# Turning each gathered tile once, in place, in a routed expert layer on one NeuronCore

## The chip, the cores and the metric

One NeuronCore of a Trainium2 chip runs the whole program. The metric is the device time of one execution in microseconds (us). PE is TensorE, DVE VectorE, ACT ScalarE, POOL GpSimd, and SP the queue that issues most DMAs.

## The reference

x has the shape (32, 32, 256), all float32. Each of the 32 sequences picks a 32x32 matrix by its index and is mixed by it; the 1024 tokens of width 256 that come out (y) go through a mixture of experts, and the result is added to x.

```python
w = weights[conditions]                        # 200 matrices of 32x32, one picked per sequence
y = einsum('bct,bcd->bdt', x, w)               # 1024 tokens, width 256
probs = softmax(y @ w_router)                  # 16 experts
top_w, top_i = top_k(probs, 4); top_w /= sum(top_w)
g = silu(y @ we1[e]) * (y @ we3[e])            # each chosen expert, hidden width 128
moe = sum over the 4 of  top_w * (g @ we2[e])
shared = silu(y @ ws1) * (y @ ws3) @ ws2       # hidden width 512
out = x + shared / 5 + moe * 4 / 5
```

## The kernel before

**Routing.** y is computed, the experts' logits and the four choices per token are found, and every (token, choice) gets a slot in an order sorted by expert. The 4096 slots make 32 *tiles* of 128 rows. POOL gathers them, `xs[:, j, :]` for tile j, by one indirect DMA each (L433) from y in DRAM (`y_of`). A tile may hold rows of several experts, so the work goes by *items*: an item is a tile with one expert, and there are 47 of them in the tiles' order, run in 24 pairs. The tile and the expert of an item are known only at run time (`item_t_i`, `item_e_i`), so engines load them into registers (`load`, a TENSOR_LOAD in the profile) and address by register.

**The loop of pairs.** All engines run `for i in range(PAIRS + LAG)` (27 rounds) with a pipeline by round. Pair n's steps, and the lines at which the profile shows them:

- SP copies the two gathered tiles of an item pair from `xs` into a ring `xt` of three pairs (`copy_pair`, L372), 128 KB each, addressed by register; for pairs 0 and 1 ACT does this (L526). Item j of a tile that has several experts copies that tile again.
- PE transposes each copied tile (`turn_pair`, L945, two 128x128 blocks a tile) into `xt_ps`, a PSUM bank for each of two pairs, in round n (t_turned).
- ACT copies x to `x_hi` in a reduced float format (L541), and DVE computes `x_lo = x - x_hi` (L752), in round n. The first four pairs (PLAIN) use x as it is, in buffers `x_f`.
- PE multiplies with the expert's two first weights (gate and up), in three products of high and low parts (L992; L986 for plain pairs), in round n + 1; ACT takes silu of the gate (L545) and DVE multiplies it by up (L757).
- In round n + 3 PE transposes that product (L970), ACT copies it to `gt` (L537), PE multiplies with the second weight (L1008, "down"), and DVE adds the rows that belong to the item into `merged` (L786, a register address each).

`merged` and `xs` are views of one store: tile m of `merged` lies on tile m - 16 of `xs`. DVE clears two tiles of `merged` a round from round 4 to 15 (L767). POOL scatters each finished tile of `merged` to DRAM (L440) after all gathers are issued.

**Weights.** Each expert's gate and up weights are loaded into `raw`, then ACT makes the high part (L466) and DVE the low part (L605, w_lo), in the order of ORDER; `SPLIT` and `HI_BEHIND` say behind which round. The last four units, 16 to 19, reuse buffers of the plain experts. Their loads are behind the copies of pairs 8, 9, 11 and 13 in SP's queue (LOAD_BEHIND), and each waits for `t_gate_up` 4, which is when the plain rounds are over.

**Gates.** POOL's gather of tile j waits until pair (j - LEAD) // 2 - 1 is turned, with LEAD 6. In rounds 17 and 18 ACT also writes four diagonal matrices each (L552), which PE uses at the end.

**After the loop.** PE does two more units of the shared expert (L894, L907); SP loads the scattered results back by token once the last scatter has landed; ACT, DVE and PE weigh and add them, and the output is stored.

In the loop the order on each engine is that of the code: PE has turn, transposed product, gate/up, down; ACT has gt, x, silu, weight; DVE has x_lo, g, weight, clear, merge.

Of the kernel before, what the change touches and what calls it, by code (L numbers as in the profile page):

```python
# [16 lines left out]
P = 128  # L17
# [3 lines left out]
def adaln_ffn(nc, x, itok, cond_w, w_router, we1, we3, we2, ws1, ws3, ws2, out):  # L21
# [21 lines left out]
    RING = 3  # L43
    LAG = 3
    SRING = 4
# [4 lines left out]
    LEAD = 6  # L50

    EARLY = 2

    LOAD_BEHIND = {8: UNITS - 2, 9: UNITS - 1, 11: UNITS, 13: UNITS + 1}


# [4 lines left out]
    LO_FRONT = [15, 2, 3, 4, 5, 6, 7, 8]  # L61
# [15 lines left out]
    with ExitStack() as ctx:  # L77
# [19 lines left out]
        xt = sb("xt", [P, RING, 2, D])  # L97
# [42 lines left out]
        def early(first, tiles):  # L140
# [32 lines left out]
        raw_at = ([xt[:, k, :, :].rearrange("p i d -> p (i d)") for k in range(FRONT)] + [raw[:, k, :] for k in range(E - LATE)]  # L173
                  + [xt[:, FRONT, :, :].rearrange("p i d -> p (i d)")] + [raw[:, k, :] for k in range(4)])
# [72 lines left out]
        xt_out = sem("xt_out")  # L247
        xt_in = [sem(f"xt_in{r}") for r in range(RING)]
        t_cleared = sem("t_cleared")
        t_turned = sem("t_turned")  # L250
        t_x_hi = sem("t_x_hi")
# [72 lines left out]
        def _(sp):  # L324
# [29 lines left out]
            registers = {}  # L354

            def copy_pair(n):

                if n == EARLY or n % 6 == 0:
                    some = range(2 * n, 2 * (n // 6 + 1) * 6)
                    values = [sp.alloc_register(f"tile{j}") for j in some]  # L360
                    sp.wait_ge(items_done, 1)
                    sp.load(values, item_t_i[0:1, some[0]:some[-1] + 1])
                    registers.update({j: sp.snap(v, donate=True, min_val=0, max_val=TILES - 1) for j, v in zip(some, values)})
                if n >= RING:
                    sp.wait_ge(t_turned, n - RING + 1)
                else:
                    sp.wait_ge(dve_lo, n + 1)
                for i in range(halves(n)):
                    j = 2 * n + i
                    if j < TILES:  # L370
                        sp.wait_ge(tile_in[j % TT], 16 * (j // TT + 1))
                    sp.dma_start(xt[:, n % RING, i, :],  # L372
                                 xs[:, bass.ds(registers[j], 1), :].rearrange("p a d -> p (a d)")).then_inc(xt_in[n % RING], 16)
# [72 lines left out]
        def _(act):  # L446
# [71 lines left out]
            registers = [act.alloc_register(f"early{j}") for j in range(2 * EARLY)]  # L518
            act.wait_ge(items_done, 1)
            act.load(registers, item_t_i[0:1, 0:2 * EARLY])  # L520
            tiles = [act.snap(v, donate=True, min_val=0, max_val=TILES - 1) for v in registers]
# [48 lines left out]
        def _(dve):  # L570
# [150 lines left out]
            low(LO_FRONT[0])  # L721
            gated(3)
            for n in LO_FRONT[1:]:
                low(n)
# [23 lines left out]
            for i in range(PAIRS + LAG):  # L748
                if (n := pair_at(i, 0)) is not None and n >= PLAIN:
# [18 lines left out]
                if i % 6 == 1 and (first := 2 * (i - 1)) < ITEMS_UP:  # L768

                    registers = [dve.alloc_register(f"merge{first + n}") for n in range(12)]  # L770
                    dve.wait_ge(items_done, 4)
                    dve.load(registers, item_t_i[0:1, first:first + 12])
# [280 lines left out]
```

## Time and profile before

| | |
|---|---|
| time, median of 3 runs | 149.15 us (148.77 to 152.94) |
| profiled execution | 150.12 us, of which the span of instructions is 148.4 us |
| TensorE clock granted, mean over the span | 0.976 |
| busy: PE / DVE / ACT / POOL | 135.7 / 105.4 / 70.5 / 65.9 us |
| loop of pairs, from the first transposes to the last merge | some 43 to 121 us |

The span runs from the first to the last instruction; what the time has beyond it lies around the program. An engine is busy while an instruction of its own runs; issuing a DMA and loading a register are not counted as busy. The chain is the row of work that ended last, followed back from the end.

### The profile page before, as it was taken

The page shows a single profiled execution, that of the slowest core. Times are in us where ns is not written, and L with a number is a line of the kernel's source. Part 1 is how long each engine was busy: PE and PEld are TensorE (multiplying, and loading weights), DVE is VectorE, ACT ScalarE, POOL GpSimd, SP SyncE. Part 2 cuts the span into 40 slices and gives each one's busy share as a digit, 9 for nine tenths or more (in the row PEclk, how much of TensorE's full clock was granted, in tenths as well). Part 3 has the DMA queues.
Part 4 walks back from the last instruction along what each step waited for, and adds up shares of the span by engine and source line. Part 5 has one row for each costly group of instructions (what it writes and reads, how often), then busy time and mean ns, then how long its engine had stood idle before and what let it go on. Part 6 is the DMA issues. An engine that isn't in the chain of part 4 may idle for free.

```text
span 148.4 us, 2809 instructions
## 1 busy us (share of the span) xinstructions
PE 135.7 (91%) x816; PEld 115.7 (78%) x816; DVE 105.4 (71%) x274; ACT 70.5 (47%) x162; POOL 65.9 (44%) x79
## 2 busy tenths in 40 slices
PE   5999999899889999998799999999999999995920
PEld 3459978688677789997799999999999878884810
DVE  4175777997939997775988989766766551119992
ACT  4046248999354544435344544485543221198000
POOL 3400000003778777775557766776576774000000
PEclk9999959999999999999999999999999999999995
DMA  3659989995335667788767665555432222799324
GB/s 99 224 139 254 261 273 289 352 328 163 104 108 172 207 176 192 208 248 274 210 200 204 228 215 173 190 198 186 175 110 106 81 101 106 247 410 414 130 71 141
DMA packets 22413, 29.55 MB, mean 199 GB/s; under 512 B 2912, under 2 KB 19168, under 8 KB 22272
## 3 DMA queue, kind: packets, MB, share of 16 engines
q1 hardware_dynamic: 18848, 19.67, 40.5%
q0 software_dynamic: 3120, 8.52, 19.0%
q10 hardware_dynamic: 432, 1.20, 2.3%
q8 instruction: 7, 0.11, 0.4%
q14 instruction: 6, 0.05, 0.1%
HBM read 17.45 MB, written 6.29 MB: 160 GB/s over the span
## 4 chain that ended last, share of the span: by engine, by line
PE 59%; DVE 14%; DMA 11%; POOL 5%; issue 4%; ACT 2%; DVEq 1%; POOLq 1%; SPq 0%
PE up_ps L992 17%; PE down_ps L1008 12%; PE down_ps L831 6%; PE gate_ps L945 6%; PE up_ps L986 4%; POOL store_t L433 3%; PE down_ps L970 3%; DMA raw<-in_L_ffn_we 3%; DMA raw<-result 3%; DMA xt<-store_t 2%; PE down_ps L849 2%; DVE acc L804 2%; ACT raw L557 2%; DMA store_t<-y_of,token_i 2%; PE down_ps L856 2%
## 5 line engine op out<-in xcount | busy, mean ns | idle before, releaser
L433 POOL DMA_INDIRECT store_t<-y_of,token_i x32 | 31.7, 992 | 43.1 <-DVE token_i L704 30.0
L440 POOL DMA_INDIRECT result<-store_t,back_i x32 | 31.4, 980 | 12.9 <-DVE store_t L786 7.4
L786 DVE SCALAR_TENSOR_TENSOR store_t<-down_ps,valid,store_t 128x256 f32 x47 | 21.5, 458 | 8.8 <-DVE store_t L786 4.9
L992 PE MATMUL up_ps<-w_hi,x_hi 128*128 x78 | 23.6, 303 | 1.2 <-DVE x_lo L752 1.2
L1008 PE MATMUL down_ps<-w,gt 128*128 x94 | 24.5, 381 | 0.0
L992 PE MATMUL up_ps<-w_hi,x_lo 128*128 x78 | 22.0, 282 | 0.0
L992 PE MATMUL up_ps<-w_lo,x_hi 128*128 x78 | 22.0, 282 | 0.0
L537 ACT ACTIVATE gt<-down_ps 128x256 f32<-128x256 f32 (+1 forms) x24 | 9.1, 379 | 20.6 <-PE down_ps L970 19.4
L1008 PEld LDWEIGHTS down_ps<-w,gt 128*128 128x128 f32 x94 | 16.3, 190 | 1.9 <-issue 0.5
L545 ACT ACTIVATE sil<-up_ps 128x256 f32<-128x256 f32 (+1 forms) x24 | 9.1, 379 | 16.1 <-PE up_ps L992 11.4
L992 PEld LDWEIGHTS up_ps<-w_hi,x_hi 128*128 128x128 f32 x78 | 14.8, 189 | 1.5 <-issue 1.5
L992 PEld LDWEIGHTS up_ps<-w_hi,x_lo 128*128 128x128 f32 x78 | 14.8, 190 | 0.0
L992 PEld LDWEIGHTS up_ps<-w_lo,x_hi 128*128 128x128 f32 x78 | 14.8, 189 | 0.0
L945 PE MATMUL gate_ps<-ident,xt 128*128 128x128 f32 x94 | 14.2, 273 | 0.5 <-DMA xt<-store_t 0.5
L752 DVE TENSOR_TENSOR x_lo<-gate_ps,x_hi 128x512 fp32r<-128x512 f32 (+1 forms) x20 | 13.4, 671 | 1.6 <-ACT x_hi L541 1.1
L945 PEld LDWEIGHTS gate_ps<-ident,xt 128*128 128x128 f32 x94 | 11.7, 141 | 3.3 <-DMA xt<-store_t 0.9
L605 DVE TENSOR_TENSOR w_lo<-raw,w_hi 128x512 fp32r<-128x512 f32 x17 | 11.1, 691 | 1.4 <-ACT w_hi L466 1.3
L757 DVE TENSOR_TENSOR g<-sil,up_ps 128x256 f32<-128x256 f32 (+1 forms) x24 | 9.8, 410 | 3.1 <-ACT sil L545 3.1
L620 DVE TENSOR_TENSOR g<-sil,up_ps 128x512 f32<-128x512 f32 x8 | 5.5, 684 | 8.9 <-PE up_ps L894 6.6
L541 ACT ACTIVATE x_hi<-gate_ps 128x512 fp32r<-128x512 f32 (+1 forms) x20 | 11.7, 583 | 0.0
L466 ACT ACTIVATE w_hi<-raw 128x512 fp32r<-128x512 f32 x17 | 10.1, 620 | 1.1 <-DMA raw<-in_L_ffn_we 1.1
L831 PE MATMUL down_ps<-sil 128*128 128x512 f32 x16 | 8.7, 707 | 1.5 <-DVE sil L571 1.5
(154 smaller groups left out, 244.8 us busy)
## 6 DMA issues: line engine op xcount, KB each, us to landing
xt<-store_t SPq DMA_DIRECT2D x43, 128.0 KB
raw<-in_L_ffn_we SPq DMA_DIRECT2D x30, 128.0 KB, 3.4
w<-in_L_ffn_we SPq DMA_DIRECT2D x4, 512.0 KB, 6.8
raw<-result SPq DMA_DIRECT2D x4, 512.0 KB, 5.1
w_lo<-result SPq DMA_DIRECT2D x4, 512.0 KB, 8.2
acc<-in_x SPq DMA_DIRECT2D x2, 512.0 KB, 4.3
y_of<-store_t ACTq DMA_DIRECT2D x1, 1024.0 KB, 6.1
out<-acc SPq DMA_DIRECT2D x3, 256.0 KB, 2.1
```

Source lines behind the costliest of these rows:

```text
L433: pool.indirect_dma_start(xs[:, j, :], None, y_of, bass.IndirectOffsetOnAxis(ap=token_i[:, j:j + 1], axis=0),).then_inc(tile_in[j % TT], 16)
L440: pool.indirect_dma_start(result, bass.IndirectOffsetOnAxis(ap=back_i[:, j:j + 1], axis=0), merged[:, j, :], None,).then_inc(result_out[j ...
L466: act.activation(high_of(n), raw_at[n], ACT.Copy).then_inc(act_hi, 1)
L541: act.activation((x_hi[:, b, :, :] if n >= PLAIN else x_f[b])[:, 0:m, :], xt_ps[b][:, 0:m, :], ACT.Copy).then_inc(t_x_hi, 1)
L605: dve.tensor_tensor(low_of(n), raw_at[n], high_of(n).bitcast(F32), ALU.subtract).then_inc(dve_lo, 1)
L752: dve.tensor_tensor(x_lo[:, b, 0:m, :], xt_ps[b][:, 0:m, :], x_hi[:, b, 0:m, :].bitcast(F32), ALU.subtract).then_inc(t_x_lo, 1)
L757: dve.tensor_tensor(t_gated[:, b, 0:m, :], t_sil[:, b, 0:m, :], gu_ps[b][:, 0:m, H:2 * H], ALU.mult).then_inc(t_g, 1)
L786: dve.scalar_tensor_tensor(out=into, in0=out_ps[n % 2][:, h, :], scalar=valid[:, it:it + 1], in1=into, op0=ALU.mult, op1=ALU.add).then_inc ...
L831: pe.matmul(row_ps[0][:, :], warm[:, 0:P], warm, start=True, stop=True)
L945: last = pe.transpose(xt_ps[b][:, h, k * P:(k + 1) * P], xt[:, r, h, k * P:(k + 1) * P], ident[:, :])
L992: last = pe.matmul(gu_ps[b][:, h, :], (x_hi, x_lo)[a][:, b, h, k * P:(k + 1) * P], pair_of(w, experts[h], k), start=(m == 0), stop=(m == 3 ...
L1008: last = pe.matmul(out_ps[b][:, h, :], gt[:, b, h, :], w2_of(experts[2 + h]), start=True, stop=True)
```

## The change

PE now transposes each gathered tile once, straight out of `xs`, two tiles a time (TURNS = 16 pairs of tiles), one pair ahead of the loop: `turn_pair(0)` and `turn_pair(1)` before it, `turn_pair(i + 1)` in round i up to round 14. ACT copies the turned pair back over the gathered tiles (`keep`, in `xs`). x_hi, x_f and x_lo are then taken from `xs` for each item by register: two operations of 128x256 on ACT and two on DVE for a pair, instead of one of 128x512 each. SP's copies, ACT's early copies and the ring `xt` go; its room becomes `first_raw`. ACT loads 12 tile registers before the loop and at the ends of rounds 5, 11 and 17; DVE loads its 12 at the starts of rounds 0, 6, 12 and 18 instead of inside rounds 1, 7, 13 and 19. The four late weights are loaded directly behind the second weights in SP's queue. LEAD becomes 10, and three weight splits on DVE (LO_FRONT) go ahead of the g of shared step 3.

```diff
-    RING = 3
     LAG = 3
+    TURNS = TILES // 2
+    GROUP = 6
...
-    LEAD = 6
-
-    EARLY = 2
-
-    LOAD_BEHIND = {8: UNITS - 2, 9: UNITS - 1, 11: UNITS, 13: UNITS + 1}
+    LEAD = 10
...
-    LO_FRONT = [15, 2, 3, 4, 5, 6, 7, 8]
+    LO_FRONT = [15, 2, 3, 4]
+    LO_THEN = [5, 6, 7, 8]
...
+        def x_of(t):
+            return xs[:, bass.ds(t, 1), :].rearrange("p a d -> p (a d)")
...
-            for n in range(EARLY, PAIRS):
-                copy_pair(n)
-                if n in LOAD_BEHIND:
-                    load(LOAD_BEHIND[n])
+            for n in range(UNITS - 2, UNITS + 2):
+                load(n)
...
+            def load_tiles(i):
+                registers = [act.alloc_register(f"turned{2 * i + j}") for j in range(2 * GROUP)]
+                act.load(registers, item_t_i[0:1, 2 * i:2 * (i + GROUP)])
+                tiles.extend(act.snap(r, donate=True, min_val=0, max_val=TILES - 1) for r in registers)
+
+            def keep(n):
+                act.wait_ge(t_turned, n + 1)
+                act.activation(xs[:, 2 * n:2 * n + 2, :], xt_ps[n % 2], ACT.Copy).then_inc(t_kept, 1)
+
             act.wait_ge(items_done, 1)
-            act.load(registers, item_t_i[0:1, 0:2 * EARLY])
...
-            for n in range(EARLY):
-                act.wait_ge(dve_lo, n + 1)
-                for j in range(2 * n, 2 * n + 2):
-                    act.wait_ge(tile_in[j], 16)
-                    act.activation(xt[:, n, j % 2, :], xs[:, bass.ds(tiles[j], 1), :].rearrange("p a d -> p (a d)"), ACT.Copy).then_inc(xt_out, 1)
+            load_tiles(0)
+            keep(0)
             for n in HI_BEHIND[-1]:
                 high(n)
...
                 if (n := pair_at(i, 0)) is not None:
-                    b, m = n % 2, halves(n)
-                    act.wait_ge(t_turned, n + 1)
-                    act.activation((x_hi[:, b, :, :] if n >= PLAIN else x_f[b])[:, 0:m, :], xt_ps[b][:, 0:m, :], ACT.Copy).then_inc(t_x_hi, 1)
+                    act.wait_ge(t_kept, min(n + 1, TURNS))
+                    for h in range(halves(n)):
+                        act.activation((x_hi[:, n % 2, :, :] if n >= PLAIN else x_f[n % 2])[:, h, :], x_of(tiles[2 * n + h]), ACT.Copy).then_inc(t_x_hi, 1)
+                if i + 1 < TURNS:
+                    keep(i + 1)
...
+                if i % GROUP == GROUP - 1 and i + 1 < PAIRS:
+                    load_tiles(i + 1)
...
-            low(LO_FRONT[0])
+            for n in LO_FRONT:
+                low(n)
             gated(3)
-            for n in LO_FRONT[1:]:
+            for n in LO_THEN:
                 low(n)
...
             for i in range(PAIRS + LAG):
+                if i % GROUP == 0 and i < PAIRS:
+                    registers = [dve.alloc_register(f"merge{2 * i + j}") for j in range(2 * GROUP)]
+                    dve.wait_ge(items_done, 4)
+                    dve.load(registers, item_t_i[0:1, 2 * i:2 * (i + GROUP)])
...
                 if (n := pair_at(i, 0)) is not None and n >= PLAIN:
-                    b, m = n % 2, halves(n)
-                    dve.wait_ge(t_x_hi, n + 1)
-                    dve.tensor_tensor(x_lo[:, b, 0:m, :], xt_ps[b][:, 0:m, :], x_hi[:, b, 0:m, :].bitcast(F32),
-                                      ALU.subtract).then_inc(t_x_lo, 1)
+                    for h in range(halves(n)):
+                        dve.wait_ge(t_x_hi, 2 * n + h + 1)
+                        dve.tensor_tensor(x_lo[:, n % 2, h, :], x_of(tiles[2 * n + h]), x_hi[:, n % 2, h, :].bitcast(F32),
+                                          ALU.subtract).then_inc(t_x_lo, 1)
...
-                    dve.wait_ge(t_turned, i + 1)
...
             def turn_pair(n):
-                r, b = n % RING, n % 2
-                if n < EARLY:
-                    pe.wait_ge(xt_out, 2 * n + 2)
-                else:
-                    pe.wait_ge(xt_in[r], 16 * (2 * (n // RING - (r < EARLY)) + halves(n)))
+                b = n % 2
+                for h in range(2):
+                    pe.wait_ge(tile_in[(2 * n + h) % TT], 16 * ((2 * n + h) // TT + 1))
                 if n < 2:
                     pe.wait_ge(silu_done, STEPS - 1 + n)
-                for h in range(halves(n)):
+                else:
+                    pe.wait_ge(t_kept, n - 1)
+                for h in range(2):
                     for k in range(KD):
-                        last = pe.transpose(xt_ps[b][:, h, k * P:(k + 1) * P], xt[:, r, h, k * P:(k + 1) * P], ident[:, :])
+                        last = pe.transpose(xt_ps[b][:, h, k * P:(k + 1) * P], xs[:, 2 * n + h, k * P:(k + 1) * P], ident[:, :])
                 last.then_inc(t_turned, 1)
...
             turn_pair(0)
             down(3)
+            turn_pair(1)
             for i in range(PAIRS + LAG):
-                if (n := pair_at(i, 0)) is not None and n:
-                    turn_pair(n)
+                if 0 < i < TURNS - 1:
+                    turn_pair(i + 1)
```

## Rows read from the trace of the kernel before

**Rows 1.** The page, the chain that ended last, share of the span by engine.

```profile
PE 59%; DVE 14%; DMA 11%; POOL 5%; issue 4%; ACT 2%; DVEq 1%; POOLq 1%; SPq 0%
```

**Rows 2.** The chain in order of time (start, us, what): one settled round, round 24's start.

```profile
88.60 0.44 PE gate_ps L945 x4
89.04 0.22 PE down_ps L970 x2
89.26 1.43 PE up_ps L992 x12
90.68 0.87 PE down_ps L1008 x4
...
114.92 0.22 PE down_ps L970 x2
```

**Rows 3.** PE's timeline: start, us, instructions, and in brackets idle time before and releaser.

```profile
48.51 0.66 PE L945 MATMUL gate_ps<-ident,xt 128*128 128x128 f32 x4 [0.52 <-DMA xt<-store_t]
...
54.88 1.89 PE L986 MATMUL up_ps<-raw,g 128*128 x8
...
71.32 0.38 PE L992 MATMUL up_ps<-w_hi,x_hi 128*128 x1 [1.23 <-DVE x_lo L752]
```

**Rows 4.** The chain in order of time: the two DMAs behind those waits.

```profile
44.95 3.52 DMA xt<-store_t
...
63.07 4.00 DMA raw<-in_L_ffn_we
```

**Rows 5.** Busy time in PE's round 9: stretch, its length, each engine, clock, DMA.

```profile
69.27:73.71 4.44, 3.21 (x24) 2.82 (x23) 3.83 (x9) 1.54 (x4) 2.51 (x3) 1.00 0.74 227
```

**Rows 6.** DVE's timeline: the g of step 3, then from one x_lo to the next.

```profile
43.09 0.69 DVE L620 TENSOR_TENSOR g<-sil,up_ps 128x512 f32<-128x512 f32 x1 [2.25 <-PE down_ps L907]
...
70.49 0.68 DVE L752 TENSOR_TENSOR x_lo<-gate_ps,x_hi 128x512 fp32r<-128x512 f32 x1
71.09 0.41 DVE L757 TENSOR_TENSOR g<-sil,up_ps 128x256 f32<-128x256 f32 x1
...
72.93 0.68 DVE L752 TENSOR_TENSOR x_lo<-gate_ps,x_hi 128x512 fp32r<-128x512 f32 x1
```

**Rows 7.** Groups by line and shape: busy us, mean ns of one, idle before.

```profile
L605 DVE TENSOR_TENSOR w_lo<-raw,w_hi 128x512 fp32r<-128x512 f32 x17 | 11.1, 691 | 1.4 <-ACT w_hi L466 1.3
L757 DVE TENSOR_TENSOR g<-sil,up_ps 128x256 f32<-128x256 f32 x23 | 9.6, 416 | 3.1 <-ACT sil L545 3.1
L526 ACT ACTIVATE xt<-store_t 128x256 f32 x4 | 1.5, 412 | 3.0 <-DVE valid L719 2.4 <-DMA store_t<-y_of,token_i 0.6
```

**Rows 8.** ACT's timeline: the first late weight, then round 17's diagonals, gt and x.

```profile
67.09 0.63 ACT L466 ACTIVATE w_hi<-raw 128x512 fp32r<-128x512 f32 x1 [1.05 <-DMA raw<-in_L_ffn_we]
...
96.89 1.26 ACT L552 ACTIVATE store_t<-ident,top_w 128x128 f32<-128x128 f32 x4
98.13 0.39 ACT L537 ACTIVATE gt<-down_ps 128x256 f32<-128x256 f32 x1
98.41 0.59 ACT L541 ACTIVATE x_hi<-gate_ps 128x512 fp32r<-128x512 f32 x1
```

**Rows 9.** Register loads by line: four registers on ACT, twelve on DVE (ns min/median/max).

```profile
L520 ACTq TENSOR_LOAD <-item_t_i x1: 501/501/501, 39.6 to 39.6; - x1
...
L772 DVEq TENSOR_LOAD <-item_t_i x4: 1005/1162/1520, 48.5 to 102.9; - x4
```

**Rows 10.** The gathers: tile 9's in POOL's timeline, and all landings by line L433.

```profile
47.35 0.95 POOL L433 DMA_INDIRECT store_t<-y_of,token_i  x1 [0.30 <-issue]
...
DMA to landing us min/median/max: 2.7/3.4/5.3
```

**Rows 11.** POOL's timeline: three of the scatters.

```profile
83.12 1.23 POOL L440 DMA_INDIRECT result<-store_t,back_i  x1 [0.30 <-issue]
...
115.82 0.97 POOL L440 DMA_INDIRECT result<-store_t,back_i  x1 [0.50 <-DVE store_t L786]
...
123.47 0.97 POOL L440 DMA_INDIRECT result<-store_t,back_i  x1 [0.30 <-issue]
```

More of the change, by code:

```diff
@@ L96, in adaln_ffn @@
         raw = sb("raw", [P, E - LATE, WC])
-        xt = sb("xt", [P, RING, 2, D])
+        first_raw = sb("first_raw", [P, FRONT + 1, WC])
         w_2 = sb("w_2", [P, E + FRONT, D])
@@ L170, in adaln_ffn @@
             "p (m n) -> p m n", m=4)
-        raw_at = ([xt[:, k, :, :].rearrange("p i d -> p (i d)") for k in range(FRONT)] + [raw[:, k, :] for k in range(E - LATE)]
-                  + [xt[:, FRONT, :, :].rearrange("p i d -> p (i d)")] + [raw[:, k, :] for k in range(4)])
+        raw_at = ([first_raw[:, k, :] for k in range(FRONT)] + [raw[:, k, :] for k in range(E - LATE)]
+                  + [first_raw[:, FRONT, :]] + [raw[:, k, :] for k in range(4)])
         x_f = [v[:, :, HALF - D:HALF] for v in (sil, g)]
@@ L246, in adaln_ffn @@
         tile_in = [sem(f"tile_in{r}") for r in range(TT)]
-        xt_out = sem("xt_out")
-        xt_in = [sem(f"xt_in{r}") for r in range(RING)]
         t_cleared = sem("t_cleared")
         t_turned = sem("t_turned")
+        t_kept = sem("t_kept")
         t_x_hi = sem("t_x_hi")
@@ L353, in _ @@
                 sp.dma_start(w_2[:, e, :], we2[e].rearrange("e h d -> h e d")).then_inc(w_2_in, 16)
[L354 to L365, printed above, removed]
-                else:
[L367 to L373, printed above, removed]
-            for n in range(EARLY, PAIRS):
-                copy_pair(n)
-                if n in LOAD_BEHIND:
-                    load(LOAD_BEHIND[n])
+            for n in range(UNITS - 2, UNITS + 2):
+                load(n)
             sp.wait_ge(dve_lo, turn[FRONT + 4] + 1)
@@ L516, in _ @@
                         zero(m)
-            registers = [act.alloc_register(f"early{j}") for j in range(2 * EARLY)]
-            act.wait_ge(items_done, 1)
-            act.load(registers, item_t_i[0:1, 0:2 * EARLY])
-            tiles = [act.snap(v, donate=True, min_val=0, max_val=TILES - 1) for v in registers]
-            for n in range(EARLY):
-                act.wait_ge(dve_lo, n + 1)
-                for j in range(2 * n, 2 * n + 2):
-                    act.wait_ge(tile_in[j], 16)
-                    act.activation(xt[:, n, j % 2, :], xs[:, bass.ds(tiles[j], 1), :].rearrange("p a d -> p (a d)"), ACT.Copy).then_inc(xt_out, 1)
+            tiles = []
+            def load_tiles(i):
[5 more added lines that the diff above has]
+                act.activation(xs[:, 2 * n:2 * n + 2, :], xt_ps[n % 2], ACT.Copy).then_inc(t_kept, 1)
+            act.wait_ge(items_done, 1)
+            load_tiles(0)
+            keep(0)
             for n in HI_BEHIND[-1]:
@@ L748, in _ @@
             for i in range(PAIRS + LAG):
+                if i % GROUP == 0 and i < PAIRS:
+                    registers = [dve.alloc_register(f"merge{2 * i + j}") for j in range(2 * GROUP)]
+                    dve.wait_ge(items_done, 4)
+                    dve.load(registers, item_t_i[0:1, 2 * i:2 * (i + GROUP)])
+                    tiles += [dve.snap(r, donate=True, min_val=0, max_val=TILES - 1) for r in registers]
                 if (n := pair_at(i, 0)) is not None and n >= PLAIN:
-                    b, m = n % 2, halves(n)
-                    dve.wait_ge(t_x_hi, n + 1)
-                    dve.tensor_tensor(x_lo[:, b, 0:m, :], xt_ps[b][:, 0:m, :], x_hi[:, b, 0:m, :].bitcast(F32),
-                                      ALU.subtract).then_inc(t_x_lo, 1)
+                    for h in range(halves(n)):
+                        dve.wait_ge(t_x_hi, 2 * n + h + 1)
+                        dve.tensor_tensor(x_lo[:, n % 2, h, :], x_of(tiles[2 * n + h]), x_hi[:, n % 2, h, :].bitcast(F32),
+                                          ALU.subtract).then_inc(t_x_lo, 1)
                 if (n := pair_at(i, 1)) is not None:
@@ L764, in _ @@
                 if ZEROED <= i < TILES // 2:
-                    dve.wait_ge(t_turned, i + 1)
                     dve.memset(merged[:, 2 * i:2 * i + 2, :], 0.0).then_inc(t_cleared, 1)
[L768 to L772, printed above, removed]
-                    tiles += [dve.snap(r, donate=True, min_val=0, max_val=TILES - 1) for r in registers]
                 if (n := pair_at(i, LAG)) is not None:
@@ L974, in _ @@
                     if n < PLAIN:
-                        pe.wait_ge(t_x_hi, n + 1)
+                        pe.wait_ge(t_x_hi, 2 * n + halves(n))
                     else:
-                        pe.wait_ge(t_x_lo, n - PLAIN + 1)
+                        pe.wait_ge(t_x_lo, 2 * (n - PLAIN) + halves(n))
                     if n == PLAIN:
```

1 line of the change is left out of this document (removed).

## The prediction

> **What bounds the kernel now.** I read the page's chain first, then the chain in order of time over the loop of item pairs, then each engine's timeline in a few rounds, and last the tail. PE carries the chain for 59% of the span [rows 1]. In the loop a settled round on the chain is four transposes of x (0.44 us), two of the gated product (0.22), twelve gate/up matmuls (1.43) and four down matmuls (0.87): 2.95 us, with nothing between them [rows 2]. So a round costs what PE executes in it, and what leaves PE leaves the round, until another engine takes over. Two waits break this: 0.52 us before the transposes of pair 2, and 1.23 us before the gate/up of pair 8 [rows 3]. The first ends with a row copy that took 3.52 us to land, the second with a late expert weight whose load was issued only at 63 us [rows 4]; that round took 4.44 us [rows 5] instead of 2.95. DVE has little room: where it waits for no other engine it needs 2.44 us from one split of x to the next [rows 6], and in rounds 7, 9, 12 and 14 it splits a weight as well.
>
> **The change, part by part.** Round i means pass i of the loop.
>
> *Fewer transposes.* There are 47 items in 23.5 pairs, but 32 tiles in 16 pairs. Each pair turned costs 0.44 us of PE [rows 2], so 7.5 pairs fewer give 3.3 us. It falls in the rounds from 15 on, which become 2.95 - 0.44 = 2.51 us; before that PE does the same four transposes a round, one pair earlier.
>
> *No row copies.* SP's 43 copies go, and with them the 0.52 us in front of pair 2 [rows 3]. What is late next at that place is the gather itself: PE now turns pair i+1 in round i and so needs tile 2i+3. Tile 9, whose gather starts at 47.35, lands 2.7 to 5.3 us later [rows 10], at 50.1 to 52.7. PE wants it in round 3, near 50.8: the 48.51 of now, less 0.52, plus one more pair (0.44), a plain gate/up (1.89) [rows 3] and another pair (0.44). At the median landing of 3.4 PE waits almost nothing, at the worst 2 us, and once: two gathers are issued in 2.5 us, a round is longer. I take nothing, and keep 0 to 2 for the range. POOL's gate is loosened too (LEAD 10): at 1.25 apart, with a few longer ones, the 22 gathers after tile 9 are through near 77 us. Nobody waits for SP in the loop any more but for late weights.
>
> *Late weights at once.* They now wait only for the end of the plain gate/ups (54.88 + 1.89, [rows 3]) and for their buffers' splits, not behind the copies of pairs 8 to 13. Eight issues at some 0.4 us each and 4.0 to land [rows 4] bring the first unit at about 61.5 and the last near 64; ACT first wanted one at 66.0 [rows 8]. The 4.44 - 2.95 = 1.5 us [rows 2, 5] go. Their 1 MB now meets the gathers of rounds 5 to 7, which by then have about 1 us of lead; that is within the 0 to 2 above.
>
> *VectorE at the loop's start.* Three weight splits move ahead of the g of step 3. DVE sat idle there for 2.25 us until PE's down was done [rows 6], and three splits take 2.1 at 0.69 [rows 7]: covered. Without that cover PE's last down would start up to 2.1 later. ACT now waits for the first transposes with the high part of unit 10 queued behind; that is read two splits later.
>
> Gross gain: 3.3 + 0.5 + 1.5 = 5.3 us. Against it stand the new steps on ACT and DVE.
>
> *ScalarE.* It gains the copy of each turned pair from PSUM in place, a 128x512 like the x copy of now, 0.59 [rows 8], and its one x copy becomes two from SBUF with a register address: L526 is that operation, at 0.41 us [rows 7]. Issue to issue such a copy takes between 0.28 [rows 8] and that; I take 0.34. A round's work is 0.28 + 0.68 + 0.59 + 0.28 = 1.83 against 2.95. By order: the product's transposes end 0.66 into PE's round, then come their copy, two parts, the kept copy and silu, which ends near 2.75. Behind the new wait on t_turned are queued silu, which DVE's g waits for, and in some rounds a weight copy; the next round's copy is wanted at 3.6, so all of it is hidden. A load of 12 registers is bounded by 0.5 (four on ACT) and 1.0 to 1.5 (twelve on DVE) [rows 9], I take 1.1; in rounds 5 and 11 it fits. In rounds 17 and 18 it doesn't: PE's rounds are 2.51 there, ACT has 1.24 for copies and silu, 1.26 for four diagonals [rows 8], and in 17 the load. The copy that down(15) waits for comes about 0.5 us late. Bounds: 0 and 1.5.
>
> *VectorE.* The split of x (0.60 from issue to issue [rows 6]) becomes two of 128x256, each with its own wait and register operation. Its price lies between 0.30 each, half of the old one, and 0.42, the duration of g at that size [rows 7], plus 0.11 for the register operation: 0 to 0.46 more a round. DVE runs behind PE there, so its queue is filled and these steps overlap; I take 0.11, near the low end, so a round of 2.55. The load of 12 registers now stands right before the split of x. It takes 1.0 to 1.5 [rows 9], of which the merge still running covers 0.4; I take 0.7. From the split of pair 6 to that of pair 16, ten rounds: 25.5, four weight splits at 0.69 [rows 7] 2.8, the routing weights 0.7, one load 0.7: 29.7 us. PE's time between the gate/ups of these pairs: eight rounds of 2.95, two of 2.51, less 0.44, since no turning stands ahead of the last: 28.2. At pair 6 DVE is some 0.7 ahead (silu ends 2.75 into a round and the merges start 0.5 into the next; 1.0 for them, load 0.7, split 0.7: 2.9 against the 3.6 at which PE wants it). So PE waits 29.7 - 28.2 - 0.7 = 0.8 us in rounds 13 to 16. With the bounds' ends: none, or 4 to 5.
>
> By the Trainium skill, DMA: Bandwidth & Descriptors, "Latency and other measured facts", a tensor load has a floor near 600 ns. The rows agree for four registers (501 ns) but show about twice that for twelve [rows 9], so the rows are used; at the page's figure most of DVE's load would be covered, and the gain would be some 0.5 larger.
>
> *Net:* 5.3 - 0.5 - 0.8 = 4.0 us.
>
> **Does the tail keep it?** After the loop the end hangs on POOL's last scatter, the loads of the results and DVE's sums. POOL last waited for a merge at 115.82, 0.9 after round 24 began [rows 2, 11], and then issued six more, 1.275 apart. Round 24 comes 4.0 earlier, so this moves as a whole, and the shared steps with it. POOL's own floor is 77 + 31 x 1.275 = 116.5 for the last issue, 7 us ahead of 123.47 [rows 11]; it doesn't bind at a gain of 4.
>
> The profiled execution took 150.12 us, 148.4 of it the span; minus 4.0 it gives 146.1. The median of the runs, 149.15, lies 1.0 lower, so I forecast 145.1.
>
> **Rivals.**
> - *Nothing new waits*: DVE's and ACT's steps stay covered; 149.15 - 5.3 = 143.8. For it: ACT's 1.83 and DVE's 2.55 are under a round. Against: DVE's weight splits and loads come on top.
> - *DVE becomes the bound* in rounds 6 to 16: the halves don't overlap (0.46 more a round, not 0.11) and a load costs 1.1. That is 10 x 0.35 + 0.4 = 3.9 on top of the forecast: 149.0; half of it, 147. For it: each half has its own wait and address. Against: a register operation fits beside the instruction that is running.
> - *The split of x slows POOL* (the other side). x's split now reads two inputs from SBUF instead of one from there and one from PSUM. The only operation of that kind in the loop is the weight split; the scatter beside one, at 83.12, took 1.23 us instead of 0.97 [rows 11]. If every scatter lost 0.35, the last would be issued at 77 + 31 x 1.625 = 127.4, 3.9 later than now: 153. It decides from a pitch of 1.50, (123.47 - 77)/31. Against: the gather at 47.35, beside weight splits too, took its usual 0.95 [rows 10]. The Trainium skill, SBUF — State Buffer, "Who interferes with whom", has such a rule: a VectorE instruction with two SBUF inputs contends with a GpSimd instruction that reads SBUF. By that rule the time would go this way; the trace agrees in one of these two rows.
> - *Gathers are late*: PE waits up to 2 us in rounds 2 to 7: 147.
>
> **How the numbers follow.** The forecast's own case (144 to 146.1): 0.52. Nothing new waits: 0.13. DVE the bound, or gathers at full price: 0.27. POOL slowed: 0.08. Two per cent is 3 us (146.2 and 152.1), about what can be told from no change here. Of the third case nearly all lies between these. Faster 0.65, same 0.27, slower 0.08. Range: from 143.3 (no new wait, and 0.5 of the median's own spread) to 148.5, which leaves out the dearest part of the DVE case and POOL's.
>
> **What would show it.** 64 transposes of x, none after round 14; rounds of 2.95 before and about 2.5 after; no wait for a weight at pair 8; PE waits for x_lo in rounds 13 to 16 and for gt at 18; the last scatter issued near 119.5. It is wrong if x's halves take clearly more than 0.35 from issue to issue, if PE's transposes wait for gathers, or if scatters stand over 1.3 us apart without waiting for a merge.

## The result, and the profile after

The changed kernel takes **147.14 us** (median of 4 runs, 146.93 to 151.51) beside 149.27 for the kernel before in the same comparison: a ratio of **0.9864, 95% interval 0.9824 to 0.9903**. (All ratios here leave out executions of either kernel that the chip had disturbed.) So it is faster, clear of the noise, but by 2.1 us where the forecast said 4.0. The time lies inside the range, but above 146.2; it is among the cases "within 2%". Measured twice more, on other chips, the same kernel gave ratios of 0.991 and 0.9885 (below), so the gain is 1.4 to 2.1 us.

The profiled execution took 147.29 us, 145.2 of it the span. The page's chain, which answers to [rows 1]: TensorE's share fell from 59% to 52%, VectorE's rose from 14% to 26%.

```profile
PE 52%; DVE 26%; issue 7%; DMA 4%; ACT 3%; DVEq 2%; POOL 1%; POOLq 1%; ACTq 0%; SPq 0%
```

The chain in order of time (start, us, what), for [rows 2 and 3]. The four transposes (L928) end with round 14; a round of 2.95 us (60.36 to 63.31) becomes one of 2.52 (108.73 to 111.25). Before the transposes of pair 3 (tiles 6 and 7) there is a new wait of 0.95 us.

```profile
47.45 0.95 issue
48.40 0.63 PE gate_ps L928 x4
...
60.36 0.44 PE gate_ps L928 x4
60.80 0.22 PE down_ps L954 x2
61.02 1.43 PE up_ps L976 x12
62.44 0.87 PE down_ps L992 x4
63.31 0.44 PE gate_ps L928 x4
...
108.73 0.22 PE down_ps L954 x2
108.95 1.44 PE up_ps L976 x12
110.38 0.87 PE down_ps L992 x4
111.25 0.22 PE down_ps L954 x2
```

The chain calls this wait "issue", because the profile names no releaser for it. The gather's own rows show what ended it (by line L408, tile 7 alone): it was issued at 43.49 and landed 4.82 us later, at 48.31. The transposes of pair 3 start 0.09 behind that, at 48.40.

```profile
L408 POOL DMA_INDIRECT store_t<-y_of,token_i x1: 1342/1342/1342, 43.5 to 43.5; - x1
...
DMA to landing us min/median/max: 4.8/4.8/4.8
```

Stretches of TensorE's rounds 6 and 9 (length, busy time of PE, PEld, DVE, ACT, POOL, clock, DMA share, GB/s), for [rows 5]: round 9 is now 2.94 long, where it was 4.44.

```profile
60.36:63.31 2.95, 2.95 (x25) 2.79 (x23) 2.09 (x7) 1.81 (x5) 2.32 (x3) 1.00 0.89 248
...
69.20:72.14 2.94, 2.94 (x25) 2.78 (x23) 2.68 (x8) 2.25 (x6) 2.33 (x3) 1.00 0.33 109
```

VectorE's timeline, for [rows 6]. With nothing to wait for, it needs 2.51 us from one split of x to the next (68.48 to 70.99; the forecast took 2.55). At 80.92 it stands 0.77 us: the registers of round 12 are being loaded.

```profile
68.48 0.75 DVE L742 TENSOR_TENSOR x_lo<-store_t,x_hi 128x256 fp32r<-128x256 f32 x2
...
70.99 0.75 DVE L742 TENSOR_TENSOR x_lo<-store_t,x_hi 128x256 fp32r<-128x256 f32 x2
...
80.92 0.76 DVE L742 TENSOR_TENSOR x_lo<-store_t,x_hi 128x256 fp32r<-128x256 f32 x2 [0.77 <-issue]
...
92.22 0.75 DVE L742 TENSOR_TENSOR x_lo<-store_t,x_hi 128x256 fp32r<-128x256 f32 x2
```

By line, for [rows 9 and 10] (ns or us, min/median/max): VectorE's and ScalarE's register loads, and the gathers' landings.

```profile
L737 DVEq TENSOR_LOAD <-item_t_i x4: 849/953/1099, 42.3 to 96.6; - x4
...
L497 ACTq TENSOR_LOAD <-item_t_i x4: 782/792/967, 38.6 to 94.9; - x4
...
DMA to landing us min/median/max: 2.6/2.9/5.3
```

GpSimd's scatters, for [rows 11]. Before, GpSimd still waited for a merge at 115.82, six scatters from the end. Now its last real wait is at 89.38; 24 scatters follow, 1.28 us apart with 0.30 idle between them, to the last. Two of them, at 94.48 and 110.01, took 1.18 and 1.22 instead of 0.97, so that the next came 1.5 behind.

```profile
83.71 0.97 POOL L415 DMA_INDIRECT result<-store_t,back_i  x1 [1.52 <-DVE store_t L769]
...
89.38 0.97 POOL L415 DMA_INDIRECT result<-store_t,back_i  x1 [0.87 <-DVE store_t L769]
90.66 0.97 POOL L415 DMA_INDIRECT result<-store_t,back_i  x1 [0.30 <-issue]
...
94.48 1.18 POOL L415 DMA_INDIRECT result<-store_t,back_i  x1 [0.30 <-DVE store_t L769]
95.97 0.97 POOL L415 DMA_INDIRECT result<-store_t,back_i  x1 [0.30 <-issue]
...
110.01 1.22 POOL L415 DMA_INDIRECT result<-store_t,back_i  x1 [0.31 <-issue]
...
120.45 0.97 POOL L415 DMA_INDIRECT result<-store_t,back_i  x1 [0.30 <-issue]
```

Both stand beside a split of x, which now reads both of its inputs from SBUF (VectorE's timeline):

```profile
94.40 0.75 DVE L742 TENSOR_TENSOR x_lo<-store_t,x_hi 128x256 fp32r<-128x256 f32 x2
...
109.96 0.42 DVE L742 TENSOR_TENSOR x_lo<-store_t,x_hi 128x256 fp32r<-128x256 f32 x1
```

**Where the gain went.** The stage ahead of the loop varies by some 1.3 us from one execution to the next (last section), so I measure from the loop's first transposes (L928, at 41.81 here, 42.79 before). The transposes of the gated product in round 24 stand 69.27 us behind them, before 71.96; the last scatter stands 78.64 behind, before 80.68. The loop gives 2.69 up to round 24 instead of 4.0, and 0.65 of that is lost between round 24 and the last scatter (9.37 us, before 8.72). What is left, 2.04, is close to the 2.1 of the medians.

### The profile page after: what moved, and what is told of

Read it like the earlier page. It is cut to its first block, busy times and chain, and to the rows that moved or that the text cites. A ratio compares the mean times of both kernels' runs of the same rounds, so it can differ in the third digit from the quotient of the medians.

```text
span 145.2 us, 2793 instructions
## 1 busy us (share of the span) xinstructions
PE 132.2 (91%) x786; PEld 111.6 (77%) x786; DVE 105.9 (73%) x293; ACT 78.8 (54%) x197; POOL 67.1 (46%) x79
## 4 chain that ended last, share of the span: by engine, by line
PE 52%; DVE 26%; issue 7%; DMA 4%; ACT 3%; DVEq 2%; POOL 1%; POOLq 1%; ACTq 0%; SPq 0%
PE up_ps L976 13%; PE down_ps L992 10%; PE down_ps L814 6%; PE down_ps L890 5%; PE up_ps L970 5%; PE gate_ps L928 3%; DVE store_t L769 3%; DMA raw<-result 3%; PE down_ps L954 2%; PE down_ps L832 2%; DVE acc L787 2%; ACT raw L541 2%; DVE x_lo L742 2%; DVE store_t L756 2%; DMA result<-store_t,back_i 2%
## 5 line engine op out<-in xcount | busy, mean ns | idle before, releaser
L408 POOL DMA_INDIRECT store_t<-y_of,token_i x32 | 32.5, 1014 | 38.5 <-DVE token_i L688 29.0
L742 DVE TENSOR_TENSOR x_lo<-store_t,x_hi 128x256 fp32r<-128x256 f32 x39 | 14.8, 420 | 2.2 <-ACT x_hi L521 1.3
L521 ACT ACTIVATE x_hi<-store_t 128x256 fp32r x39 | 14.0, 408 | 0.0
L502 ACT ACTIVATE store_t<-gate_ps 128x512 f32<-128x512 f32 x16 | 9.4, 590 | 6.8 <-PE gate_ps L928 6.8
L814 PE MATMUL down_ps<-sil 128*128 128x512 f32 x16 | 9.3, 747 | 1.5 <-DVE sil L555 1.5
L928 PE MATMUL gate_ps<-ident,store_t 128*128 128x128 f32 x64 | 9.5, 273 | 0.9 <-issue 0.9
```

The source lines that it names most:

```text
L408: pool.indirect_dma_start(xs[:, j, :], None, y_of, bass.IndirectOffsetOnAxis(ap=token_i[:, j:j + 1], axis=0),).then_inc(tile_in[j % TT], 16)
L521: act.activation((x_hi[:, n % 2, :, :] if n >= PLAIN else x_f[n % 2])[:, h, :], x_of(tiles[2 * n + h]), ACT.Copy).then_inc(t_x_hi, 1)
L742: dve.tensor_tensor(x_lo[:, n % 2, h, :], x_of(tiles[2 * n + h]), x_hi[:, n % 2, h, :].bitcast(F32), ALU.subtract).then_inc(t_x_lo, 1)
L814: pe.matmul(row_ps[0][:, :], warm[:, 0:P], warm, start=True, stop=True)
L928: last = pe.transpose(xt_ps[b][:, h, k * P:(k + 1) * P], xs[:, 2 * n + h, k * P:(k + 1) * P], ident[:, :])
```

## The experiments

Theory, before these runs: the four microseconds were there, and three new waits took half: gathers that land late, VectorE in rounds 12 to 17, GpSimd's own pace at the end. Rivals: the late weights at once were needed for the gain in round 9; the split of x slows GpSimd; the tail keeps whatever the loop gains. All kernels but one (the late weights alone) start from the changed one. "R24" and "last" are the distances of round 24's transposes and of the last scatter from the loop's start, in the profiled execution (changed kernel 69.27 and 78.64).

**Turning behind gate and up.** It gives every gather some 1.65 us more, the 0.22 and 1.43 of the steps that now stand ahead.

```diff
-                if 0 < i < TURNS - 1:
-                    turn_pair(i + 1)
...
                     last.then_inc(t_gate_up, 1)
+                if 0 < i < TURNS - 1:
+                    turn_pair(i + 1)
```

> The changed kernel, with PE turning the next pair of tiles after the gate/up of a round instead of ahead of it, and ACT keeping it after silu. Theory: the 0.95 us that PE stands before the turning of pair 3 is the gather of tile 7, which the change asks for one pair sooner than it lands; with the gate/up of pair 1 in front the gather has time, the wait goes, every later round and scatter starts earlier by it: 146.3 us, 0.8 below the changed kernel. Rival: the wait is absorbed later anyway, since DVE is late in rounds 12 to 16: 147.1, no change.

Ratio 0.9968 (0.9925 to 1.0011), R24 69.78: in time nearly all of the gain is gone, though to round 24 its profile is only 0.5 behind the changed kernel's; the loop also starts 0.97 later in this profile (last section). No wait at pair 3 (8.16 us to round 3 instead of 9.38, with one turning, 0.44, fewer in it), but now rounds 9, 11, 12, 13, 14 and 16 are long, by 2.5 us together; in the changed kernel that is 1.2. ScalarE's copies of turned pairs were moved behind silu here too, so two things changed. A narrower form moves the turning in rounds 1 to 3 only, ScalarE's order as it was; a control is the changed kernel once more, on the same chip.

> The changed kernel once more, unaltered, as the base for the three beside it on the same chip. 147.1 us as first measured, or up to 148 if part of that gain came from the stage before the loop, whose length differed by 1 us between the two first traces (first transposes at 42.8 against 41.8).

> The changed kernel, with PE turning after the gate/up in rounds 1 to 3 only, and ACT's order as it was. The first edit of this kind also changed ACT's order and the lead of every later round. Theory: PE's stand before the turning of pair 3 (0.95) goes, the split of pair 6 comes 0.7 earlier, and from there on all moves as a whole: 0.7 us below the changed kernel of this call. Rival: DVE and POOL are bound from round 6 on by work that doesn't start earlier, PE's waits for x_lo in rounds 13 to 17 grow by what is saved: within 0.2 of it.

Control 148.03 us, ratio 0.991 (0.9857 to 0.9962), R24 69.23; the narrower form 147.51, 0.9896 (0.985 to 0.9941), R24 68.51. The control has no wait at pair 3 this time, but rounds 6 and 7 are longer by 0.21 and 0.64: a transposition of L928 at 66.25 stands 0.44 us, and the gather of its tile 19 had landed at 66.16. So the place of the wait changes from run to run, which a fixed cost of the new order wouldn't. The times alone don't separate the two kernels.

**Late weights.** First alone, on the kernel before:

```diff
-    LOAD_BEHIND = {8: UNITS - 2, 9: UNITS - 1, 11: UNITS, 13: UNITS + 1}
+    LOAD_BEHIND = {6: UNITS - 2, 7: UNITS - 1, 8: UNITS, 9: UNITS + 1}
```

> The kernel before with one part of the change alone: the loads of the four late weights stand behind the copies of pairs 6 to 9 instead of 8, 9, 11 and 13. Theory: the 1.5 us of round 9 go and nothing takes their place: 147.7 us, PE without a wait at pair 8. Rival: DVE and SP's queue, now busy with weights between copies, make PE wait elsewhere (copies late): 148.8 to 149.3.

Ratio 0.9991 (0.9949 to 1.0034). Round 9 falls from 4.43 to 3.11, but rounds 6 to 9 each take 0.09 to 0.20 more than a settled one; R24 71.11, 0.85 earlier than before, of which the median shows 0.1; where the rest goes isn't traced. Then three of the four loads later again, on the changed kernel:

```diff
-            for n in range(UNITS - 2, UNITS + 2):
+            for n, turned in ((UNITS - 2, 7), (UNITS - 1, 8), (UNITS, 10), (UNITS + 1, 12)):
+                sp.wait_ge(t_turned, turned)
                 load(n)
```

> The changed kernel with one part undone: the four late weights are issued behind turnings 7, 8, 10 and 12, about when they were before. Theory: PE's wait for the weight at pair 8 comes back and delays DVE, the bound of the rounds behind it: 1.2 to 1.5 us above the changed kernel of this call. Rival: PE waits there, but the waits of rounds 13 to 17 get shorter by as much: under 0.5 above.

146.98 us, ratio 0.9841 (0.9789 to 0.9893), R24 68.36, against 148.03 for the control beside it. No wait at pair 8 (round 9: 2.94), and none for a gather. The edit doesn't make the first unit late again, as was expected: seven pairs are turned as early as round 5, and SP issues this load at 56.8, beside 56.6 in the changed kernel, 56.9 with the late weights alone and 62.7 before. The other three go at 59.7, 65.6 and 71.5. So the rival is out for these three, which needn't go at once. What takes the wait at pair 8 away in all three kernels is that the first unit goes some 6 us earlier.

**VectorE.** The clears of `merged` leave it for ScalarE, a round later:

```diff
-                if ZEROED <= i < TILES // 2:
-                    dve.memset(merged[:, 2 * i:2 * i + 2, :], 0.0).then_inc(t_cleared, 1)
...
+                if ZEROED <= (m := i - 1) < TILES // 2:
+                    if m >= E // 2:
+                        act.wait_ge(t_x_lo, 2 * (m - PLAIN) + 2)
+                    act.activation(merged[:, 2 * m:2 * m + 2, :], ..., ACT.Copy, scale=0.0).then_inc(t_cleared, 1)
```

> The changed kernel, with the 12 clears of merged moved from DVE to ACT, one round later. Theory: DVE is the bound of rounds 12 to 16, where PE waits 1.2 us for x_lo in all; 0.4 us a round off DVE takes these waits away, the merges of rounds 11 to 14 come over 1 us earlier, and POOL's row of scatters, which runs without a wait from tile 7 on, starts earlier with them: 146.0 us. Rival: POOL's own floor (gathers through at 76.3, 32 scatters at 1.275) or ACT, now at 2.4 us a round, is next: 147.0 or more.

146.58 us, ratio 0.9824 (0.9745 to 0.9903), R24 68.19, last 77.08. Rounds 12 to 15 are 2.95, 2.95, 2.51 and 2.52 with no wait for x_lo; round 16 keeps 0.22. With the first edit added:

> The changed kernel with both edits, turning after gate/up and clears on ACT. Theory: the two waits are separate, so the gains add: 145.2 us. Rival: they cover one another, since POOL's scatters bind: 146.0, as with the better of the two.

146.86 us, 0.9838 (0.9741 to 0.9935), R24 68.29: nothing on top. The run with the clears alone had lost only 0.3 at the start, and the first edit, with ScalarE's new order, costs about as much again: round 13 is 0.05 longer, round 16 0.43 instead of 0.22.

**GpSimd's pace.** Leaving scatters out needs something in their rows: a control fills the results with 4 MB behind the last weights (SyncE, and GpSimd waits for it), then the next run leaves out the scatters of tiles 12 to 15, so that these rows hold the fill and the output is not the reference's.

```diff
+            for part_of in range(2):
+                sp.dma_start(result...[part_of], w_2[:, 0:E, :]).then_inc(prefilled, 16)
...
             pool.wait_ge(back_done, 1)
+            pool.wait_ge(prefilled, 32)
```

> A control for the next run: the changed kernel, and SyncE fills the array of results behind its last weights with 4 MB that are overwritten later; GpSimd's first scatter waits for that. Both theories: loop as in the changed kernel or up to 1 us longer by the added transfers, last scatter 78.4 to 79.6 us behind the start of the loop, scatters without a wait 1.275 us apart behind tile 7 or so. Median 147 to 148.5.

> The control with the scatters of tiles 12 to 15 left out, so that their rows of the result keep what was filled in. Theory (behind the last merge that it waits for, GpSimd runs at its own 1.275 us a scatter, and 0.65 us of the savings are lost there): GpSimd catches up by up to 5.1 us and then waits for merges again; the last scatter stands 0.5 to 0.8 us earlier against round 24 than in the control (8.7 us behind its transposes of gt in place of 9.4), and the median is 0.4 to 0.8 below the control. Rival (the last merge sets the last scatter): the same place of the last scatter within 0.15 us, and the same time.

Control 149.53 us, ratio 0.9983 (0.9925 to 1.0042); four fewer 148.91, 0.995 (0.9912 to 0.9989). GpSimd's timeline with four fewer: it waits for merges again at 102.75 and 104.65.

```profile
97.06 1.19 POOL L423 DMA_INDIRECT result<-store_t,back_i  x1 [0.30 <-issue]
102.75 1.13 POOL L423 DMA_INDIRECT result<-store_t,back_i  x1 [4.50 <-DVE store_t L777]
104.65 0.96 POOL L423 DMA_INDIRECT result<-store_t,back_i  x1 [0.77 <-DVE store_t L777]
...
122.51 0.97 POOL L423 DMA_INDIRECT result<-store_t,back_i  x1 [0.30 <-issue]
```

From round 24 (113.67) that is 8.84 us; in the control 9.37, as in the changed kernel (112.69 to 122.06). So GpSimd's row of scatters, and not the last merge, held the end back by 0.53; the time is 0.62 lower, though the intervals overlap. This run doesn't tell the usual pace of 1.28 from the two slowed scatters, which also stand in the control (1.18 and 1.23). The control shows a second thing: the fill is a larger burst beside the gathers. Gathers of tiles 20 and 21 take 7.0 and 7.2 us to land and round 8 takes 4.57; with four scatters fewer it is round 7, at 5.36. TensorE stands at two transpositions (the control's timeline). The first starts 0.09 behind the landing of tile 21, at 69.95; the second is that of the gated product, no gather's, and its cause isn't shown.

```profile
70.04 0.63 PE L933 MATMUL gate_ps<-ident,store_t 128*128 128x128 f32 x4 [0.79 <-issue]
...
71.15 0.41 PE L959 MATMUL down_ps<-ident,g 128*128 128x128 f32 x2 [0.48 <-issue]
```

**Mends together.** Three: clears on ScalarE, turning behind gate and up in rounds 1 to 3, and the diagonals behind the loop; then with the late weights spread too (four mends); then only clears and spread weights.

```diff
-                if i >= DIAG_ROUND and i - DIAG_ROUND < len(PE_TILES):
...
             for s in range(STEPS, LAST_STEP - 1):
                 shared_silu(s)
+                if s - STEPS < len(PE_TILES):
```

> The changed kernel with clears on ACT, turning after the gate/up in rounds 1 to 3, and ACT's eight diagonals moved from rounds 17 and 18 to the shared units behind the loop. With the clears on ACT, PE waited only at pair 4's turning (0.39) and for gt in rounds 17 and 18 (0.45 each). Theory: both go, POOL's scatters then follow the merges to about tile 25 again: 1.2 us below the kernel with clears on ACT alone, 145.4 us. Rival: POOL, which ran without a wait from tile 15 on there, keeps its pace and only 0.4 is gained: 146.2.

> The changed kernel with four edits: the clears of merged on ScalarE a round later; the turning behind gate and up in rounds 1 to 3; the diagonals behind the loop; the late weights again behind the turning of pairs 7, 8, 10 and 12. Theory (the lost gain lies in gathers that land late, in VectorE as the bound of rounds 12 to 17, and the 1 MB of late weights at once is itself what makes gathers of rounds 6 and 7 late): no wait of TensorE over 0.3 us ahead of a turning in rounds 3 to 9, none for x_lo, round 24 67.5 to 68.2 us behind the start of the loop (before 71.96, changed 69.25), median 144.9 to 145.7, about 0.7 below the three mends with the weights at once (146.23). Rival (spreading costs the wait for weights of pair 8 that the change removed): a wait of about 1.2 us at pair 8, median 146.9 or more.

> The changed kernel with the clears of merged on ScalarE and the late weights again behind the turning of pairs 7, 8, 10 and 12; nothing else. Theory: the two gains lie in different rounds (6 to 9 and 12 to 17) and add: clears alone gave 0.56 below the changed kernel, spreading alone 1.05 below its own control, so 145.4 to 146.0. A wait for a gather at pair 3 or 4 may stay (0.4 to 1.0 us). Rival (the last scatters are bound by GpSimd's own pace, so that TensorE's gains beyond one of them are lost): the same as clears alone, 146.5, with the last scatter no earlier than 77.1 us behind the start of the loop.

Ratios 0.979 (0.9684 to 0.9896), 0.9808 (0.9756 to 0.986) and 0.9809 (0.9766 to 0.9852); medians 146.23, 146.3 and 145.73. The first has a round 7 of 4.21 us (1.07 of it ahead of pair 9's turning, where a gather is awaited), the other two have none. The three missed their 145.4. The four met their place of round 24 (67.96) and missed their 144.9 to 145.7; to round 24 the third, without the later turning and with the diagonals where they were, stands at 67.86. So the diagonals gave nothing. With them in rounds 17 and 18, rounds 18 and 19 take 2.98 and 3.00, so 0.94 over 2.52 each; without them 2.52 and 3.46, the same 0.94. VectorE's timeline with the four mends shows why: the load of registers of round 18, which the diagonals had hidden.

```profile
96.19 0.48 DVE L772 SCALAR_TENSOR_TENSOR store_t<-down_ps,valid,store_t 128x256 f32 x1 [0.21 <-DVE store_t L772]
97.49 0.80 DVE L748 TENSOR_TENSOR x_lo<-store_t,x_hi 128x256 fp32r<-128x256 f32 x2 [0.81 <-issue]
```

**A square on one chip**: the changed kernel, weights spread, clears on ScalarE, both. All four have been seen above, on other chips.

> The changed kernel as it is, the corner of a square of four on one chip. Both theories: 147 to 148.

> The late weights spread behind the turning of pairs 7, 8, 10, 12, nothing else. Theory (the burst makes gathers late): 0.5 to 1.1 below the corner. Rival (chance between calls): within 0.3 of it.

> The clears on ScalarE, nothing else. Theory (VectorE is the bound of rounds 12 to 17): 0.4 to 1.0 below the corner. Rival: within 0.3.

> Both. Theory (they act in different rounds): the sum of the two, 1.0 to 2.0 below the corner. Rival (GpSimd's pace at the end takes what comes beyond one of them): no lower than the better one.

| | ratio to before | R24 | last | rounds 6 and 7 |
|---|---|---|---|---|
| changed | 0.9885 (0.9815 to 0.9954) | 69.68 | 79.05 | 2.94, 4.22 |
| spread | 0.9821 (0.9759 to 0.9882) | 68.39 | 77.77 | 2.95, 2.94 |
| clears | 0.9818 (0.9758 to 0.9879) | 69.14 | 77.96 | 3.05, 4.13 |
| both | 0.9779 (0.9713 to 0.9845) | 67.85 | 76.68 | 2.95, 2.94 |

In the first one's profile the loop starts at 45.80, with a granted clock of 0.90 from 10 us up to there; from there to the last scatter it is 1.00, as in the others, so the distances can be compared. In these four profiles the two effects add: 1.28 and 1.09 earlier at the last scatter, 2.37 together. The ratios say 0.64, 0.67 and 1.06 per cent, with intervals as wide as that. TensorE's timeline of the third, with the weights at once:

```profile
66.17 0.63 PE L930 MATMUL gate_ps<-ident,store_t 128*128 128x128 f32 x4 [1.00 <-issue]
```

The gather of its tile 19, which that turning needs (by line L408): issued at 59.91, landed 6.17 later, at 66.08, and TensorE starts 0.09 behind that.

```profile
L408 POOL DMA_INDIRECT store_t<-y_of,token_i x1: 942/942/942, 59.9 to 59.9; - x1
...
DMA to landing us min/median/max: 6.2/6.2/6.2
```

The same tile's in the second, with the weights spread:

```profile
L409 POOL DMA_INDIRECT store_t<-y_of,token_i x1: 947/947/947, 61.4 to 61.4; - x1
...
DMA to landing us min/median/max: 3.9/3.9/3.9
```

So these waits are gathers that land late, and the burst of weights makes them late. Tile 19's gather took 5.0 to 6.2 us in the eight profiles of the changed order with the weights at once that tell it, and 3.5 and 3.9 in the two with them spread; tile 20's took 4.6 to 5.5 in seven, and 3.0 to 3.6 in three. Whether TensorE then stands is a matter of some tenths: a wait in rounds 6 or 7 stands in 4 of 9 profiles with the weights at once and no fill, and in none of 5 with them spread, too few to tell by the count alone. Both edits together take 2.2% off the kernel before on this chip; the same kernel, as the last of the mends, took 1.9% off on another.

## Why the prediction gave twice the gain

Two steps failed, the gathers at nothing and the tail that doesn't bind, and one term, VectorE's, was too small.

*Fewer transposes*: right. 64 transposes of x, none after round 14, rounds of 2.95 and 2.52.

*Late weights*: the size was right (round 9 lost 1.49), the reason only half. That the first unit goes at 56.6 instead of 62.7 brings it; sending the other three with it wasn't needed and makes gathers late.

*Gathers*: the step that failed is "I take nothing, and keep 0 to 2 for the range". I compared one landing with one demand at the median landing of 3.4 and dismissed the burst since gathers "by then have about 1 us of lead". Tile 9's demand was read rightly: in all four profiles of the square its gather lands just as TensorE wants it, 0.1 us ahead of the start of its turning, and the round is 0.02 longer. But the three profiles of the changed kernel lose 0.95 (pair 3), 0.85 (rounds 6 and 7) and 1.3 us (round 7) to other tiles, against rounds where no gather is late: each time about 1, never 0. With 32 gathers and landings from 2.6 to 6.2, the longest counts, not the median. Only the two later places are the burst's. The gather of tile 7 went at 43.5, before the late weights; why it took 4.8 there, and 3.1 to 3.4 in the nine other profiles of the changed order that tell it, stays open.

*ScalarE*: the size was right. gt came late in rounds 18 and 19, 0.31 and 0.14, together 0.45 (forecast 0.5), behind the diagonals. But it was not there to be had: with the clears moved, the two rounds lose 0.94 with the diagonals and without, since VectorE's load of registers stands behind them.

*VectorE*: the mechanism was right, the term of 0.8 too small. x's halves cost 0.67 us from issue to issue for the two (68.48 to 69.15), and from pair 6's split to pair 16's it took 62.48 to 92.22, 29.7 us as forecast. TensorE's rounds 13, 14 and 16 are longer by 0.42, 0.15 and 0.63, which is 1.2: VectorE's split of pair 6 was through 0.48 before TensorE wanted it, not 0.7, which is half of the difference. That it is VectorE, the clears show: without them these waits go, but for 0.22.

*The tail*: the sentence "it doesn't bind at a gain of 4" failed. I laid GpSimd's 32 scatters end to end from the gathers on and found room. But each also waits for its merge, and the early ones must wait: until tile 7 at 89.38. From there 24 scatters at about 1.28 stand against merges that come every 1.26 (two in a round of 2.52), so GpSimd never waits again and every delay of its own moves the end. It cost 0.65. Most of that is the two scatters beside splits of x: laid out by the trace's rows (0.28 behind its merge, or 0.30 behind the scatter before), the last one comes where it was measured, 9.37 behind round 24; with these two at 0.97 it would come at 8.91, so 0.46 of the 0.65 is theirs. That is an estimate from those rows, and no run took the two away alone. But it fits all profiles of the changed order with 32 scatters. The eight with 9.36 to 9.39 have these two slow behind their last wait. With the clears moved, the last wait is tile 15's or 17's, no scatter behind it took over 1.02, and the seven have 8.82 to 8.89. Four scatters fewer gave 0.53 back.

*Books* from the start of the loop: 4.0 forecast, less 1.0 for gathers, 0.4 for VectorE and 0.65 for GpSimd, makes 2.0; 2.04 measured in this profile. The other two of the changed kernel lose their time to gathers at other places, so that the sum closes this well is in part luck.

*Rivals*: "nothing new waits" is out; "gathers are late" came true at half its price, "VectorE the bound" at a tenth of it. That 147 stands beside two of them is chance: several terms make it. "The split of x slows POOL" came true too, at 0.46 of its 3.9: the median scatter is 0.97 before and after, but some are held up. Of the 1148 gathers and scatters in all 18 profiles, 574 ran beside no split of a weight and, in the changed order, beside no split of x either (these are VectorE's operations with two SBUF inputs there). None of these 574 took over 1.05 us to issue. Of the other 574, which ran beside one, 165 did, up to 1.49. The trace of before had five of them, each beside a weight split: four gathers, which I passed over for the one at 47.35, and the scatter at 83.12. Beside its split of x alone, which reads PSUM, 22 ran, and none was slow. The Trainium skill's rule on two SBUF inputs (SBUF — State Buffer, "Who interferes with whom"), that such a VectorE instruction contends with a GpSimd instruction that reads SBUF, is seen in this case, in 3 of the 32 scatters of the changed kernel. The price was wrong: not every scatter loses 0.35, and only what falls behind the last wait counts.

The 501 ns of four registers [rows 9] lie below the floor that the prediction quotes for a register load, so this row doesn't agree with it; nothing in the sum hangs on that.

## What to carry to other kernels

When a change shortens the distance between a transfer and its use, price the slowest of all the landings, at the place where other transfers are under way, not the median of one. When the engine that sets the rounds gets faster, lay the next engine's floor from each release on, not from its free start: a consumer that needs 1.28 a piece can't follow a producer that now gives one every 1.26, and from then on each piece that takes longer moves the end. When one row in a trace is unusually long, look for all rows like it and for what ran beside them, not for one that contradicts it. And try the parts of a change that hide a wait apart: here one of four early loads took the wait away, and the other three gave some of the gain away again.

## What was not expected of the hardware

The loop starts at 41.5 to 42.4 us in 11 profiles and at 42.8 to 43.0 in 6 (in one at 45.8), though the kernels hardly differ up to there. The stretches show it; this is the kernel with the clears on ScalarE, first run (length, busy PE, PEld, DVE, ACT, POOL, clock, DMA share, GB/s):

```profile
14.40:18.10 3.70, 3.70 (x32) 3.65 (x32) 2.46 (x12) 1.35 (x3) 0.00 (x0) 1.00 1.01 295
18.10:21.70 3.60, 3.60 (x11) 2.89 (x11) 3.39 (x24) 1.31 (x3) 0.00 (x0) 0.56 0.86 254
```

The granted clock falls to a mean of 0.56, so to the lower level (1.2 of 2.4 GHz) for most of that stretch, after TensorE had been busy without a gap, as in the profile below too; it executes 11 instructions there. The same kernel in the square, with 1.00 throughout, executes 25 and starts the loop 1.27 us earlier:

```profile
18.10:21.70 3.60, 3.60 (x25) 2.88 (x24) 3.43 (x26) 2.21 (x5) 0.00 (x0) 1.00 0.89 250
```

What makes it fall isn't settled. It fits the starts: up to 45 us the mean granted clock is 0.96 in the profile of before, which starts late, and 1.00 in that of after. Two profiles can thus differ by over a microsecond for no reason of the kernel's; the profile of before has the late start and that of after hasn't, so their spans differ by 3.2 us where the medians differ by 2.1.
